# Moving the last 36 row scatters behind the start of the expert stage, with full tiles first and pixel runs in the strided walks

## What is computed

```python
t = t + ffn(layernorm(t))
probs = softmax(xf @ Wr.T + br)
top2_prob, top2_idx = top_k(probs, 2)
h = gelu(xf @ W1[e] + b1[e]); o = h @ W2[e] + b2[e]
y = sum over the two chosen e of top2_prob * o
```

## Time and profile before

| what | value |
|---|---|
| median of 3 runs | 1658.89 us (1657.28 to 1659.47) |
| the profiled execution | 1662.11 us, span 1660.4 us |
| busy: PE, DVE, ACT, POOL | 1251.2, 1101.1, 720.6, 535.8 us |
| chain that ended last | PE 59%, DVE 11%, ACT 8%, DMA 8%, POOL 4% |
| scatters of rows (L1621) | 162, 159.0 us busy |
| returns of rows (L1630) | 176, 254.8 us busy |

### The profile page before, as it was taken

How to read it: one execution, slowest core, us unless ns; L and a number is a source line. 1 busy time by engine, 2 the same in 40 slices (tenths; PEclk the granted TensorE clock), 3 DMA queues, 4 the chain that set the end, 5 groups by cost and what they waited for, 6 DMA issues and landing times.

```text
span 1660.4 us, 36623 instructions
## 1 busy us (share of the span) xinstructions
PE 1251.2 (75%) x9504; PEld 1024.6 (62%) x9505; DVE 1101.1 (66%) x2637; ACT 720.6 (43%) x1741; POOL 535.8 (32%) x497
## 2 busy tenths in 40 slices
PE   0197879896999999997556522999999999999200
PEld 0187778892565565557545512888888888888100
DVE  7796456564778777775676672666666666666493
ACT  0293233333555555554667641333333333333350
POOL 0163111110111111110467774444454545544100
PEclk9997788887999999995555555999999999999655
DMA  8536787869878888861233444222222333222576
GB/s 314 136 91 183 243 285 282 323 240 244 192 175 184 182 185 197 197 147 53 96 131 134 140 155 130 86 86 89 89 89 84 88 92 93 90 90 70 230 284 256
DMA packets 239768, 267.87 MB, mean 161 GB/s; under 512 B 119696, under 2 KB 211988, under 8 KB 235818
## 3 DMA queue, kind: packets, MB, share of 16 engines
q1 hardware_dynamic: 219413, 214.20, 44.6%
q0 software_dynamic: 20320, 53.28, 9.6%
HBM read 158.69 MB, written 116.19 MB: 166 GB/s over the span
## 4 chain that ended last, share of the span: by engine, by line
PE 59%; DVE 11%; ACT 8%; DMA 8%; SPq 4%; issue 4%; POOL 4%; DVEq 0%; POOLq 0%; ACTq 0%
PE ps L803 15%; PE ps L788 14%; POOL rows_d L1621 4%; PE ps L596 3%; PE ps L613 3%; PE ps L562 3%; DMA u_d<-in_zstrings 3%; PE ps L627 2%; PE ps L772 2%; DVE big L1361 2%; PE ps L674 2%; PE ps L629 2%; DVE pool_ L1353 2%; PE ps L618 2%; ACT aux L1493 2%
## 5 line engine op out<-in xcount | busy, mean ns | idle before, releaser
L1630 POOL DMA_INDIRECT y_d<-pool_,to_s x176 | 254.8, 1448 | 278.7 <-DVE pool_ L1321 242.5
L803 PE MATMUL ps<-pool_,aux 128*128 x2112 | 248.7, 274 | 6.0 <-DVE aux L1313 3.4
L788 PE MATMUL ps<-aux,pool_ 128*128 128x256 f16 x2112 | 247.5, 274 | 0.6 <-ACT aux L1543 0.3
L803 PEld LDWEIGHTS ps<-pool_,aux 128*128 128x128 f16 x2112 | 199.8, 98 | 49.9 <-issue 25.3
L788 PEld LDWEIGHTS ps<-aux,pool_ 128*128 x2112 | 206.4, 98 | 25.9 <-issue 1.2
L1543 ACT ACTIVATE aux<-ps,b_s 128x256 f32<-128x256 f32 x352 | 138.3, 475 | 162.5 <-DVE aux L1313 162.0
L1621 POOL DMA_INDIRECT rows_d<-aux,idx_s x162 | 159.0, 982 | 103.4 <-DVE idx_s L1223 54.3
L1610 POOL DMA_DIRECT2D pool_<-v_d x64 | 47.9, 753 | 338.6 <-PE ps L682 323.8
L1321 DVE SCALAR_TENSOR_TENSOR pool_<-ps,pool_ 128x512 f32<-128x512 f32 x88 | 60.9, 692 | 140.6 <-PE ps L803 140.6
L1535 ACT ACTIVATE aux<-ps 128x512 f16<-128x512 f32 x88 | 52.5, 597 | 188.8 <-PE ps L772 188.8
L1313 DVE TENSOR_TENSOR aux<-aux 128x1024 f16<-128x1024 f32 x88 | 107.9, 1226 | 3.1
(11 more groups left out here) (209 smaller groups left out, 2691.2 us busy)
## 6 DMA issues: line engine op xcount, KB each, us to landing
pool_<-rows_d SPq DMA_DIRECT2D x88, 258.0 KB
pool_<-y_d SPq DMA_DIRECT2D x18, 1152.0 KB, 8.5
big<-in_x SPq DMA_DIRECT2D x2, 5184.0 KB, 21.0
xn_d<-big SPq DMA_DIRECT2D x16, 648.0 KB, 5.4
aux<-in_x SPq DMA_DIRECT2D x64, 162.0 KB, 2.9
v_d<-aux SPq DMA_DIRECT2D x64, 162.0 KB, 2.6
ks_d<-big SPq DMA_DIRECT2D x16, 648.0 KB, 3.8
pool_<-v_d POOLq DMA_DIRECT2D x64, 162.0 KB, 3.3
```

Source lines behind the costliest of these rows:

```text
L788: last = nc.tensor.matmul(o, w_s[:, a, bass.ds(e * (4 * PIECE) + (k * HID + j * 128), 128)], xh_s[:, par, b, k * SLOTS:(k + 1) * SLOTS], s ...
L803: last = nc.tensor.matmul(ps[:, 6 + par, s * C:(s + 1) * C], hh_s[:, par, a, j, s * 128:(s + 1) * 128], w_s[:, b, bass.ds(e * (4 * PIECE) ...
L1630: nc.gpsimd.indirect_dma_start(out=y_d[:, :], out_offset=bass.IndirectOffsetOnAxis(ap=to_s[:, par, k:k + 1], axis=0), in_=yo_s[:, par, k, ...
```

## The change

The scatters of the last two chunks (turns 21 to 26, `LATE` = 21) leave the router stage. POOL sends six of them (`AHEAD`) before the first tile's return, and one behind the return of each of the next 30 tiles. So that no tile needs a row that isn't there yet, the tiles that are full with rows of turns 0 to 20 (63 pixels) come first, expert by expert, and the others after them, again expert by expert; at least `FULL` tiles are of the first kind. DVE counts the full tiles between chunks 7 and 8 (`full_tiles`), and the table has 16 segments in place of 8. SP waits for scatters of turns 15 to 20 before the first load, and for those of turns 21 to 26 before the load of tile 54. ACT writes the rows of turns 24 to 26 behind the last weight piece, and DVE their places behind the table. `idx_s` has three buffers instead of two, and the expert stage's tiles in `aux` lie behind the ring, which is now still in use.

Besides, five strided walks are turned: the innermost steps go over neighbouring pixels, two or three floats side by side in `big` or `pool_`, and the other operand is walked in larger steps instead. These are L914 (k1), L1585 (x back), L1474 (tokens), L1497 (x1 turned) and L1361 (finish).

```diff
+LATE = TURNS - RING
+LATE_BATCHES = 2
+LATE_SCATTERS = RING * SUBS * 2
+AHEAD = 6
+SEGMENTS = 2 * EXPERTS
+FULL = (LATE * SUBS * BS * 2 - EXPERTS * (SLOTS - 1)) // SLOTS
...
-        idx_s = sb("idx_s", [128, 2, 2, MOST_SUBS], u32)
+        idx_s = sb("idx_s", [128, 3, 2, MOST_SUBS], u32)
...
-        aux_at[0] = 0
+        aux_at[0] = RING * SUBS * WIDE
         xh_s = take_aux(128, 2, 2, HALVES * SLOTS, dt=fp16)
...
-            for r in range(TURNS - RING, TURNS):
+            for r in range(LATE - RING, LATE):
                 sp.wait_ge(*sent(r))
...
+            with sp.Fori(1, FULL // 2 - 1) as i:
+                load_later(i)
+            for r in range(LATE, TURNS):
+                sp.wait_ge(*sent(r))
+            with sp.Fori(FULL // 2 - 1, TILES // 2 - 1) as i:
+                load_later(i)
...
-                    ins = nc.vector.tensor_tensor(by_pixel(pool_)[:, bass.ds(i * PIX + k, n), :],
-                                                  ps[:, 4 + 2 * par + k // 2, 0:n * C].rearrange("p (k c) -> p k c", k=n),
+                    ins = nc.vector.tensor_tensor(pool_.rearrange("b (c p) -> b c p", p=HW)[:, :, bass.ds(i * PIX + k, n)],
+                                                  ps[:, 4 + 2 * par + k // 2, 0:n * C].rearrange("p (k c) -> p c k", k=n),
...
+            def row_places(r):
+                if r >= RING:
+                    dve.wait_ge(*sent(r - RING))
+                    dve.sem_inc(S["settle_v"], 1)
+                return nc.vector.tensor_copy(xf_s[:, r % RING, :, C:C + 1],
+                                             pos_s[:, 0, r * SUBS:(r + 1) * SUBS].unsqueeze(2))
+            def full_tiles():
+                full, ends = seg_s[:, 0, 0:EXPERTS], seg_s[:, 2, 0:EXPERTS]
+                link(nc.vector.tensor_tensor(full, base_s[:, :], region_s[:, :], ALU.subtract))
+                link(nc.vector.tensor_copy(tili_s[:, 2, :], full))
+                link(nc.vector.tensor_scalar(tili_s[:, 2, :], tili_s[:, 2, :], SLOTS.bit_length() - 1, None,
+                                             ALU.arith_shift_right))
+                link(nc.vector.tensor_copy(full, tili_s[:, 2, :]))
+                nc.vector.tensor_copy(seg_s[:, 1, 0:EXPERTS], full)
+                link(nc.vector.tensor_copy(ends, full))
+                for e in range(1, EXPERTS):
+                    link(nc.vector.tensor_tensor(ends[:, e:e + 1], ends[:, e:e + 1], ends[:, e - 1:e], ALU.add))
+                link(nc.vector.tensor_tensor(seg_s[:, 1, EXPERTS - 1:EXPERTS], full[:, EXPERTS - 1:EXPERTS], full[:, 0:1],
+                                             ALU.subtract))
...
+                if t + 1 == len(CHUNKS) - LATE_BATCHES:
+                    full_tiles()
...
-            for e in range(1, EXPERTS):
+            for e in range(EXPERTS, SEGMENTS):
                 link(nc.vector.tensor_tensor(ends[:, e:e + 1], ends[:, e:e + 1], ends[:, e - 1:e], ALU.add))
...
-            full = [1, TILES, EXPERTS]
+            full = [1, TILES, SEGMENTS]
...
+            for r in CHUNKS[-1]:
+                row_places(r).then_inc(S["late_c"], 1)
+            for r in range(LATE - RING, LATE):
                 dve.wait_ge(*sent(r))
+            dve.wait_ge(S["xft_c"], TURNS + CREDIT)
...
-                x1 = x1_turned[:, r * SUBS:(r + 1) * SUBS, :]
+                x1 = x1_turned[:, r * SUBS:(r + 1) * SUBS, :].rearrange("b s c -> b c s")
-                nc.vector.tensor_tensor(x1, x1, got_s[:, slot, 0, at:at + SUBS, :], ALU.add).then_inc(S["fin_c"], 1)
+                nc.vector.tensor_tensor(x1, x1, got_s[:, slot, 0, at:at + SUBS, :].rearrange("b s c -> b c s"),
+                                        ALU.add).then_inc(S["fin_c"], 1)
...
-                nc.scalar.activation(xs_s[r % 3].rearrange("p h (s b) -> p h s b", s=SUBS),
-                                     x1_pixels[:, :, r * SUBS:(r + 1) * SUBS, :], ACT.Copy).then_inc(S["xs_c"], 1)
+                nc.scalar.activation(xs_s[r % 3].rearrange("p h (s b) -> p h b s", s=SUBS),
+                                     x1_pixels[:, :, :, r * SUBS:(r + 1) * SUBS], ACT.Copy).then_inc(S["xs_c"], 1)
...
-                nc.scalar.activation(x1_turned[:, r * SUBS:(r + 1) * SUBS, :],
+                nc.scalar.activation(x1_turned[:, r * SUBS:(r + 1) * SUBS, :].rearrange("b s c -> b c s"),
                                      ps[:, 2 * slot:2 * slot + 2, :].rearrange("p b n -> p (b n)")[:, 0:SUBS * C]
-                                     .rearrange("p (s c) -> p s c", s=SUBS), ACT.Copy).then_inc(S["x1t_c"], 1)
+                                     .rearrange("p (s c) -> p c s", s=SUBS), ACT.Copy).then_inc(S["x1t_c"], 1)
...
-                        rows(r)
+                        if t + 2 < len(CHUNKS):
+                            rows(r)
...
+            for r in CHUNKS[-1]:
+                rows(r)
...
-                nc.gpsimd.tensor_copy(by_pixel(big)[:, bass.ds(i * PIX, PIX), :], xp_s[:, par]).then_inc(S["xb_c"], 1)
+                nc.gpsimd.tensor_copy(big.rearrange("b (c p) -> b c p", p=HW)[:, :, bass.ds(i * PIX, PIX)],
+                                      xp_s[:, par].rearrange("b k c -> b c k")).then_inc(S["xb_c"], 1)
...
-            for t, chunks in enumerate(CHUNKS):
+            for t, chunks in enumerate(CHUNKS[:-LATE_BATCHES]):
                 pool.wait_ge(S["idx_c"], t + 1)
...
+            pool.wait_ge(S["idx_c"], len(CHUNKS))
+            pool.wait_ge(S["xft_c"], TURNS + CREDIT)
+            pool.wait_ge(S["late_c"], len(CHUNKS[-1]))
+            settle()
+            for j in range(AHEAD):
+                late_scatter(j)
+            for j in range(AHEAD, LATE_SCATTERS):
+                t = j - AHEAD
+                return_rows(t, t % 2)
+                late_scatter(j)
+            with pool.Fori((LATE_SCATTERS - AHEAD) // 2, TILES // 2) as i:
                 for par in range(2):
                     return_rows(i * 2 + par, par)
```

More of the change, by code:

```diff
@@ L486, in _, with load_later @@
                 load_rows(t + 2, t)
-            with sp.Fori(1, TILES // 2 - 1) as i:
+            def load_later(i):
                 for par in range(2):
@@ L1216, in positions @@
                 link(ins)
[L1217 to L1223, removed]
+                if t + 1 < len(CHUNKS):
+                    for r in CHUNKS[t]:
+                        row_places(r)
+                nc.vector.tensor_copy(idx_s[:, t % 3, :, 0:n], pos_s[:, :, p:p + n]).then_inc(S["idx_c"], 1)
             row_statistics(0)
@@ L1249, in _ @@
                 low_piece(n, n % 3)
-            cnt, tiles, ends = (til_s[:, k, :] for k in range(3))
+            cnt, tiles = (til_s[:, k, :] for k in range(2))
+            count, steps, ends = (seg_s[:, k, :] for k in range(3))
             link(nc.vector.tensor_tensor(cnt, base_s[:, :], region_s[0:128, :], ALU.subtract))
@@ L1256, in _ @@
             link(nc.vector.tensor_copy(tiles, tili_s[:, 0, :]))
-            link(nc.vector.tensor_copy(ends, tiles))
-            for e in range(1, EXPERTS):
+            nc.vector.memset(steps[:, SEGMENTS - 1:SEGMENTS], 0.0)
+            nc.vector.tensor_tensor(steps[:, EXPERTS:SEGMENTS - 1], tiles[:, 0:EXPERTS - 1], count[:, 1:EXPERTS], ALU.subtract)
+            link(nc.vector.tensor_tensor(ends[:, EXPERTS:SEGMENTS], tiles, count[:, 0:EXPERTS], ALU.subtract))
+            for e in range(EXPERTS, SEGMENTS):
@@ L1259, in _ @@
                 link(nc.vector.tensor_tensor(ends[:, e:e + 1], ends[:, e:e + 1], ends[:, e - 1:e], ALU.add))
-            full = [1, TILES, EXPERTS]
-            link(nc.vector.tensor_tensor(tcmp_s[:, 0], ends[0:1, :].unsqueeze(1).to_broadcast(full),
+            full = [1, TILES, SEGMENTS]
+            seg, at, live, half = (tab_s[:, k, :] for k in range(4))
+            link(nc.vector.tensor_tensor(tcmp_s, ends[0:1, :].unsqueeze(1).to_broadcast(full),
                                          turn_s[:, :].unsqueeze(2).to_broadcast(full), ALU.is_le))
-            link(nc.vector.tensor_tensor(tcmp_s[:, 1], tcmp_s[:, 0], tiles[0:1, :].unsqueeze(1).to_broadcast(full), ALU.mult))
@@ L1273, in _ @@
-            link(nc.vector.tensor_scalar(tab_s[:, 3, :], tab_s[:, 0, :], float(EXPERTS - 1), None, ALU.min))
-            link(nc.vector.tensor_copy(tabi_s[:, 0, :], tab_s[:, 2, :]))
-            nc.vector.tensor_copy(tabi_s[:, 1, :], tab_s[:, 3, :]).then_inc(S["base_c"], 1)
-            for r in range(TURNS - RING, TURNS):
+            link(nc.vector.reduce_sum(seg, tcmp_s, axis=AX.X))
+            link(nc.vector.tensor_tensor(tcmp_s, tcmp_s, steps[0:1, :].unsqueeze(1).to_broadcast(full), ALU.mult))
```

39 lines of the change are left out of this document (25 added, 14 removed).

## The result

| what | before | after |
|---|---|---|
| median of 4 runs each | 1658.85 us (1657.28 to 1659.47) | 1622.52 us (1621.29 to 1624.04) |
| profiled execution, span | 1662.11, 1660.4 us | 1624.04, 1622.3 us |
| first load of a tile | 1021.28 | 996.36 |
| first load of results | 1553.55 | 1527.81 |
| first output transfer | 1633.70 | 1595.66 |

The ratio is 0.9783, with an interval of 0.9766 to 0.98: 36.3 us less, where the forecast was 23.6 us less (1635) and its range reached down to 1617. The last three rows of the table split the gain of the spans, 38.1 us: 24.9 us lie before the first load of a tile, 0.8 in the expert stage (532.27 to 531.45), 12.3 between the first load of results and the first output transfer (80.15 to 67.85), and 0.1 behind it. They were forecast as 23.6 (0.4 of them for k1), 0, 0 and 0.

A forecast was written before the change was run, and what follows sets the result against it. GpSimd's scatters were taken to bound the expert stage's start: moving them brings it 23.2 us earlier, k1 adds 0.4, sum 23.6; 1635 us as a median, own range 1630 to 1641, down to 1617 with rival A, up to 1647 with rival B.

The forecast's parts named there:

- tokens: ACT's copy to tokens, router stage: a strided read traded for an equally dear strided write, 0 us.
- finish: DVE's 27 instructions on the path at the end: stay near 1512 ns, taken as 0; bounds 15.4 us either way.
- rival A: finish at the end gains as well, 27 x 0.57 = 15.4 us more: 1620; chance 0.22.
- I take 997.1, nearer to the row of the same instruction: Border to the expert stage: landing of the ninth zero rows, chosen between 994.1 and 998.3.
- 4.1 + 3.6 = 7.7: Router stage: x1's cheaper copy brings the last cast of places 7.7 us earlier, before and during GpSimd's full queue.
- 5.6 - 2.7 = 2.9: Last chunks: 5.6 us of DVE's weight-piece waits go, counting full tiles costs 2.7; last cast 2.9 us earlier.
- 7 x 0.58 = 4.1 us: Router stage until the scatters of chunk 2: seven x1 copies on the chain, each 0.58 us shorter.
- x1's copy: ACT's copy of x1 out of PSUM: 950 ns in place of 1530, bounds 810 and 1530.
- rival B: Runs of three stay at the strided price in x1's copy: 15.6 us gained, 1643; chance 0.13.
- The late scatters: POOL, first 30 tiles: each fits in 2.71 us of idle time, cost 0; 46.5 us if the cover failed.
- Rival C: GpSimd's queue, first 30 tiles: late scatters over 2.4 us hold up returns; at 3.7 us, 39 us and 1674; chance 0.03.
- k1 and x back: k1 on DVE gains 0.4 us, bounds 0 and 11.5; x's copy back on POOL taken as 0, 2 us if dearer.

The follow-up runs named there:

- e1: The five new walks alone in the kernel before, all 162 scatters still ahead of the expert stage: 1644.93 us, ratio 0.9907.
- e2: The changed kernel with the five old walks, so late scatters, full tiles first and the longer table alone: 1640.5 us, ratio 0.9876.
- e3: The changed kernel with the old walk in the copy of x1 alone: 1628.22 us, ratio 0.9799 to the kernel before.
- e7: The changed kernel with each of the 30 late scatters behind a return sent twice, the second time to a spare table: 1624.47 us, ratio 0.9789.
- e4: The changed kernel with the old walk in finish alone: 1635.0 us, ratio 0.9842 to the kernel before.
- e5: The changed kernel with finish walking every fourth channel first, so a result's neighbour is read 192 elements later instead of 3: 1633.8 us, ratio 0.9849.
- e8: The changed kernel with the tokens' tile laid out image by pixel and finish done over nine pixels per instruction: 1630.92 us, ratio 0.9817.
- e6: The changed kernel with the tokens' tile laid out image by pixel, so its copy writes in order: 1618.76 us, ratio 0.9755.
- e9: The changed kernel unedited, run again beside e10 and e8: 1621.25 us, ratio 0.976 to the kernel before.
- e10: The same kernel as e6 a second time, with the changed kernel beside it: 1620.83 us, ratio 0.9759 to the kernel before.

## Why the prediction was right or wrong

**What bounds, right.** The scatters set the start before; once they were moved, what follows the last places set it, and the first load came 24.9 us earlier against 23.6. The measured 1622.5 still lies outside the forecast's own range of 1630 to 1641; it is close to rival A's 1620, for the reason given under finish.

**Which of the two sets it, wrong by little.** The prediction had the zero rows land 1.1 us after the table; they land 0.6 us before it. The step "I take 997.1, nearer to the row of the same instruction" is the one: without scatters beside it the landing took 3.6 us, nearer to the other bound (2.42) than to 6.6. e1 and e2 bear this out: 6.7 us with the scatters beside it, 3.4 without. The table was ready 2.8 us later behind the last places than before (13.1 to 15.9 us) against 3.9; 0.4 us of that is a shorter wait for the last weight piece (1.17 us in place of 1.54). That piece is next in line: the prediction had the table follow the last places alone, but the chain of waits goes through the load of that piece. The zero rows land only 0.6 us before the table, so an earlier piece alone would bring no more than that.

**The last places: the sum right, its terms not.** Predicted 10.6 us earlier, measured 10.0 (989.57 to 979.55). e2 and e3, both with the old x1 copy, part the two terms: their last places lie 192.4 and 192.3 us behind their first ones, against 197.8 before and 187.2 to 188.8 with the new copy. So the copy brought 3.5 to 5.2 us against 4.1 + 3.6 = 7.7, and the move 5.4 to 5.5 against 5.6 - 2.7 = 2.9. The two errors cancel, which is luck.

- "7 x 0.58 = 4.1 us" is the failed step of the first. I carried the lead that ACT and DVE win ahead of the full queue through the whole of it, as if the scatters kept their duration. The first scatter of chunk 2 comes 2.7 us earlier, counted from the first places (833.79 - 791.75 = 42.04 and 830.64 - 791.31 = 39.33):

```profile
833.79 0.96 POOL L1621 DMA_INDIRECT rows_d<-aux,idx_s  x1 [7.63 <-DVE idx_s L1223]
```

```profile
830.64 0.95 POOL L1671 DMA_INDIRECT rows_d<-aux,idx_s  x1 [5.37 <-DVE idx_s L1258]
```

GpSimd's last early scatter starts at 970.63, the same one before at 971.01, so counted in the same way nothing of the lead is left (179.32 and 179.26): the 126 scatters took 126.5 us in place of 123.1. The scatter that the rows of turn 23 wait for started at 947.44 instead of 947.93, and landed 3.85 us later instead of the 2.42 that I took. So these rows start at 951.38, 2.6 us earlier than 953.97 and not 7.7. ACT waits for ring buffers, 12.9 us in five waits, where it had none:

```profile
947.44 3.85 DMA rows_d<-aux,idx_s
951.38 1.48 ACT aux L1539 x3
```

```profile
ACT aux L1539 <- DMA rows_d<-aux,idx_s: 12.9, 5, 3.7
```

- In the second, the rows that left the loop took more waits with them than the three I counted. Between the places of chunk 7 and the last ones DVE waited 8.8 us for weight pieces before and 3.2 after, 5.6 less as predicted, and 1.1 us in another wait for ACT is gone as well, and the copies of the last chunk's places (0.5) have moved behind the table. The count of full tiles took 2.6 us of DVE, as predicted (2.7), but not on the path: the chain of the changed kernel passes it by, from the scatter that lands at 951.29 to ACT's rows of turn 23, and DVE still waits 1.95 us for ACT behind the count (the L1151 at 954.30 above). DVE's waits in this stretch, before and then after:

```profile
DVE pool_ L1135 <- ACT pool_ L1504: 8.8, 5, 2.5
DVE aux L1154 <- ACT aux L1483: 1.1, 1, 1.1
```

```profile
DVE pool_ L1151 <- ACT pool_ L1550: 3.2, 2, 1.9
```

**x1's copy, right:** 949 ns against 950, so rival B falls. It reads PSUM in steps of 1024 B, with no two elements side by side, and the old walk with PSUM in order took 1535 in e3. The Trainium skill ("Advanced Engine Details and Errata", section Memory Cachelines) asks for best throughput that every two consecutive PSUM elements lie side by side, in a list that names matmuls. For this ACT copy the SBUF side outweighs it, at 949 against 1535, and the measurement decides; as the prediction's estimate without strides was 810, a smaller price of the PSUM read is not excluded.

**The late scatters, right at 0,** with 1.25 us left of each tile, 0.30 of it a gap (e7 uses it up). Rival C was priced by the right queue, but its threshold of 2.4 us takes off one gap where a late scatter has one on either side; with both it is 2.71 - 0.60 = 2.1. In e7 the two scatters with the gap between them take 0.96 + 0.30 + 0.96 to 1.19 = 2.2 to 2.5 us and the stage is 4.4 us longer, so the edge lies near there; e7 does not tell the two thresholds apart, as its first returns got shorter too (1.66 to 1.72 us in place of 1.93).

**k1 and x back, right.** k1 fell by 0.34 us an instruction and its share of the chain around its stage is 1.4%, 1.7% before. x back got cheaper, not dearer, and waits for ACT instead, 107.0 us in all where it was 94.3.

**finish, wrong: nearly the whole miss of 12.7 us.** "As L1474 shows that a strided read alone costs the full price, I take 0." It measured 1052 ns, neither the 1512 of the forecast nor rival A's 950: 27 x 0.46 = 12.4 us, the 12.3 between the first load of results and the first output, and the 12.5 of e4. The row was the wrong neighbour. L1474 reads single floats with the neighbour 128 elements later; the new finish reads three rows in turn, so the neighbour comes three elements later. e5 puts it off again and pays 1542; e8 has nine rows in turn and pays most of it. The case was there as rival A, and the "For it" of A (an interleaved PSUM read at no price) was the better analogy, for it was the only row with an interleaved walk. The Trainium skill ("Advanced Engine Details and Errata", section Memory Cachelines) says that SBUF is at full performance where subsequent accesses hit the same line of 16 B, and that a line needs at least two hits. Taken as accesses one right behind the other, the new finish would have no such hits among its results and stay at 1512; with two accesses in between it fell to 1052, with 191 (e5) it did not, and with eight (e8) most of the price was back. The runs agree with the rule if "subsequent" reaches over a few accesses of a read; that reading is mine, and e5 and e8 support it without showing what the engine keeps.

**tokens, right number, wrong reason.** I had the strided read traded for an equally dear strided write. e6 shows that after the change the write was the dear side (1554 to 999 with the same read).

## What to carry to other kernels

In these runs a strided walk went by when the neighbour in memory is read, not by the step: rows read in turns of three were nearly free, in turns of nine they were not, and a write in large steps stayed dear. When a queue is the bound, a faster producer ahead of it gains nothing (e1), and a lead won before the queue is full lasts only while the queue keeps its pace, while moving the queue's work under another engine's stage gains until the next thing in line; list the next two, and price both. Check a small gain beside the kernel it is compared with: e6's 3.8 us were 0.4 when both ran side by side, and 1 us in the traces.

## What was not expected of the hardware

**Slow scatters start inside a VectorE instruction that reads two tensors from SBUF.** Most scatters take GpSimd 0.96 us. In the kernel before 12 of 162 took over 1.05 (8 of the first 126), in the changed kernel 21 of its first 126. Every one of them starts while DVE runs an instruction with two tensor inputs in SBUF (the low weight piece L1151 and the products L1199 to L1201; L1135, L1183, L1185 and the table's L1265 before), and ends 0.82 to 0.85 us after that instruction does. Two such pairs, from POOL's and from DVE's timeline of the kernel before:

```profile
960.71 1.15 POOL L1621 DMA_INDIRECT rows_d<-aux,idx_s  x1 [0.30 <-issue]
998.32 1.59 POOL L1621 DMA_INDIRECT rows_d<-aux,idx_s  x1 [0.30 <-issue]
```

```profile
960.27 0.76 DVE L1185 TENSOR_TENSOR aux<-aux,lower_s 128x576 bf16<-128x576 bf16 x1
998.19 0.88 DVE L1265 TENSOR_TENSOR aux<-aux,til_s 1x704 f32<-1x704 f32 x1
```

One is of 16-bit numbers, the other of 32-bit ones, so the type does not tell them apart. A scatter that starts inside a sum over one tensor keeps its 0.96 us, here the one right behind the first pair:

```profile
962.16 0.96 POOL L1621 DMA_INDIRECT rows_d<-aux,idx_s  x1 [0.30 <-issue]
```

```profile
961.06 1.35 DVE L1188 TENSOR_REDUCE aux<-aux 128x72 f32<-128x1152 bf16 x1
```

The slow first return of a tile, which rival C named, fits too: the one at 1028.03 starts inside the split of the hidden layer (L1358, 1027.86 to 1029.09), takes 1.93 us and ends 0.87 us behind it; in e7, where the returns start later in that instruction, all but the first of the 30 take 1.66 to 1.72.

With the new walks scatters start inside such instructions more often, and earlier in them: the first 126 average 1004 ns in place of 977, 3.4 us of GpSimd's full queue, against the 2.7 us that the shorter copy had won ahead of it. e1 and e9 show the same (1009 and 1005 ns), e2 with the old walks does not (980). This is a relation in time, the same in the traces of before, after, e1, e2, e3, e9 and e10; no run took the DVE instructions away, so the cause is not shown.
